# Attention with exponentials in transit: products with v a quarter slot later over three buffers, and norm statistics on POOL instead of VectorE

## The reference, cut to what matters

```
x = x + LN(attention(LN(x)))
x = x + LN(encoder_layer(LN(x)))       # 4-head attention over 8 positions, then 8 experts with capacity
```

```
q, k, v = relu(x Wq' + bq), relu(keys Wk' + bk), relu(values Wv' + bv)      # keys, values: shared by the batch
score   = q k' / sqrt(8)                                                    # 16 heads of width 8, 512 x 512
a       = softmax(score) v
a       = transpose(a, (0, 1, 3, 2)).reshape(8, 512, 128)                   # so 4 heads make 128 tokens
```

## Time and profile before

| | |
|---|---|
| three timed runs | 621.78, 622.29, 622.56 us; median 622.29 |
| the profiled execution | 623.81 us on the device, of which the span from first to last instruction is 621.3 |
| PE busy | 510.5 us, 82% |
| DVE busy | 526.5 us, 85% |
| ACT busy | 395.3 us, 64% |
| POOL busy | 194.5 us, 31% |
| row maxima, L1665 on DVE | 256 times 1220 ns |
| exponentials, L1597 on ACT | 512 times 604 ns |
| products with v, L1492 on PE | 1024 passes |

### The profile page before, as it was taken

How to read it: one execution, slowest core, us unless ns; L and a number is a source line. 1 busy time by engine, 2 the same in 40 slices (tenths; PEclk the granted TensorE clock), 3 DMA queues, 4 the chain that set the end, 5 groups by cost and what they waited for, 6 DMA issues and landing times.

```text
span 621.3 us, 9777 instructions
## 1 busy us (share of the span) xinstructions
PE 510.5 (82%) x3468; PEld 196.5 (32%) x3475; DVE 526.5 (85%) x879; ACT 395.3 (64%) x773; POOL 194.5 (31%) x309
## 2 busy tenths in 40 slices
PE   1794799999989999999999999877768798888520
PEld 1480122222222222222222222246547664433200
DVE  4769889999999999999999996157998769899976
ACT  1643378898989888888888988525446421144252
POOL 7000212039604544043461318329456330000000
PEclk9997589999999999999999999999988899999965
DMA  9943011111221112121112200010000000000012
GB/s 232 293 141 120 24 27 30 28 38 25 69 61 46 30 32 57 49 59 37 29 36 66 64 23 9 6 50 34 1 2 1 1 1 1 1 0 28 7 34 68
DMA packets 31392, 28.93 MB, mean 47 GB/s; under 512 B 6240, under 2 KB 23784, under 8 KB 31344
## 3 DMA queue, kind: packets, MB, share of 16 engines
q1 hardware_dynamic: 29312, 27.33, 15.1%
q10 hardware_dynamic: 2032, 0.98, 0.6%
HBM read 19.23 MB, written 8.65 MB: 45 GB/s over the span
## 4 chain that ended last, share of the span: by engine, by line
PE 45%; DVE 32%; POOL 7%; ACT 7%; issue 5%; DMA 2%; ACTq 1%; SPq 0%; DVEq 0%
PE ps L1492 14%; PE ps L1487 11%; DVE row_max L1665 10%; PE ps L1460 5%; DVE space L926 4%; PE ps L585 2%; DVE space L862 2%; ACT attended L1613 2%; ACT space L1597 2%; DMA w_in<-in_L_ffn_out_proj_w 1%; DVE st L233 1%; ACT space L830 1%; POOL space L402 1%; POOL space L404 1%; PE ps L342 1%
## 5 line engine op out<-in xcount | busy, mean ns | idle before, releaser
L1665 DVE TENSOR_REDUCE row_max<-ps 128x2 f32<-128x1024 f32 x256 | 299.5, 1220 | 17.0 <-PE ps L1460 14.2
L1597 ACT ACTIVATE space<-ps 128x512 f32<-128x512 f32 x512 | 271.8, 604 | 48.3 <-PE ps L1487 47.9
L1487 PE MATMUL ps<-space 51*128 51x512 bf16 x512 | 159.2, 388 | 7.0 <-ACT space L1597 3.3
L1492 PE MATMUL ps<-space 128*32 128x512 f32 x1024 | 138.1, 612 | 2.9 <-ACT space L1597 0.7
L1460 PE MATMUL ps<-space 48*128 48x512 bf16 x512 | 128.3, 400 | 14.2 <-DVE row_max L1665 12.5
L1487 PEld LDWEIGHTS ps<-space 51*128 51x128 bf16 x512 | 41.1, 94 | 165.1 <-ACT space L1597 144.6
L1333 POOL CAST max_parts<-row_max 128x16 bf16<-128x16 f32 x32 | 6.3, 198 | 236.8 <-DVE row_max L1665 236.8
L585 PE MATMUL ps<-W,space 128*128 128x512 f32 x128 | 66.7, 603 | 0.4
L926 DVE TENSOR_REDUCE space<-ps 128x128 f32<-128x1024 f32 x32 | 38.7, 1221 | 9.1 <-PE ps L585 8.8
L448 POOL TENSOR_TENSOR space<-PC,same_row 128x512 f32<-128x512 f32 x32 | 33.0, 1064 | 35.5 <-DVE PC L876 27.4
L1460 PEld LDWEIGHTS ps<-space 48*128 48x128 bf16 x512 | 26.4, 94 | 56.1 <-DVE row_max L1665 50.2
(11 more groups left out here) (216 smaller groups left out, 623.0 us busy)
## 6 DMA issues: line engine op xcount, KB each, us to landing
q_parts_dram<-space SPq DMA_DIRECT2D x2, 1536.0 KB, 5.4
space<-q_parts_dram SPq DMA_DIRECT2D x64, 48.0 KB
attended_dram<-attended SPq DMA_DIRECT2D x128, 18.0 KB
X<-in_L_attn_queries SPq DMA_DIRECT2D x8, 256.0 KB, 7.7
space<-in_L_ffn_w SPq DMA_DIRECT2D x2, 1024.0 KB, 5.9
space<-q_parts_dram SPq DMA_DIRECT2D x64, 32.0 KB
space<-attended_dram SPq DMA_DIRECT2D x16, 128.0 KB, 2.4
space<-inverses_dram SPq DMA_DIRECT2D x16, 128.0 KB
```

Of the source, the lines that this page charges most:

```text
L1487: pe.matmul(ps[:, col_bank(v), :], k_rows[rows_a, kappa // 4 % 2, tc * P:(tc + 1) * P], q_stack[rows_a, kappa % 4, b * S:(b + 1) * S], sta ...
L1492: mm = pe.matmul(ps[32 * m:32 * m + 32, PV, :], v_heads[:, tc, PAIR * (kappa // 4) + m % PAIR, :], probs[:, tc % 2, m, :], start=(tc == 0) ...
L1597: act.activation(probs[:, tc % 2, m, :], ps[:, col_bank(v), :], ACT.Exp, scale=1.0 / math.sqrt(DH)).then_inc(s_pr, 1)
L1665: dve.tensor_reduce(row_max[:, par].rearrange("p (a c) -> p a c", a=PAIR)[:, :, item], ring(n), AX.X, MAX).then_inc(s_free, 1)
```

## The change

Six things are changed.

1. `multiply_v` in a step multiplies the quarter before; after the last step one more call follows. The exponentials have three buffers, the third over `space8`.
2. ACT copies `attended` of slot kappa - 1 inside quarter 1 of slot kappa, between the third and the fourth exponential. Before, it did so after quarter 0.
3. SP issues `load_shift` before `store_attended` in each slot.
4. The statistics of groups 0 to 2 leave DVE. POOL sums 128 features by halving (`pool_add_up`: 7 additions), subtracts the mean, squares and sums again; a norm is spread over two slots (c = 4, 5 and 6, 7).
5. The addition of the output bias moves to the next slot c = 0, or behind the loop.
6. The turn of the first slot's maxima stands two pairs of rows earlier.

```diff
-        probs = view(space4, 0, [2, QB, S])
+        probs = [view(space4, 0, [QB, S]), view(space4, QB * S, [QB, S]), view(space8, 0, [QB, S])]
...
+        def pool_add_up(pool, ch, src, scratch, total):
+            n = D // 2
+            ch.done(pool.tensor_tensor(scratch[:, :, 0:n], src[:, :, 0:n], src[:, :, n:2 * n], ADD))
+            ch.wait()
+            while n > 2:
+                n //= 2
+                ch.done(pool.tensor_tensor(scratch[:, :, 0:n], scratch[:, :, 0:n], scratch[:, :, n:2 * n], ADD))
+                ch.wait()
+            ch.done(pool.tensor_tensor(total.rearrange("p (b o) -> p b o", o=1), scratch[:, :, 0:1],
+                                       scratch[:, :, 1:2], ADD))
+            ch.wait()
+        def pool_centre(pool, ch, src, dst, scratch):
+            mean = smallp[:, 0, :]
+            pool_add_up(pool, ch, src, scratch, mean)
+            ch.done(pool.tensor_scalar(mean, mean, 1.0 / D, None, MUL))
+            ch.wait()
+            ch.done(pool.tensor_tensor(dst, src, over_f(mean), SUB))
+            ch.wait()
+            ch.done(pool.tensor_tensor(scratch, dst, dst, MUL))
+            ch.wait()
+        def pool_scale(pool, ch, dst, scratch):
+            var, inv = smallp[:, 2, :], smallp[:, 3, :]
+            pool_add_up(pool, ch, scratch, scratch, var)
             ch.done(pool.tensor_scalar(var, var, 1.0 / D, EPS, MUL, ADD))
             ch.wait()
             ch.done(pool.tensor_tensor(inv, var, neg_half[:], ALU.pow))
             ch.wait()
             return pool.tensor_tensor(dst, dst, over_f(inv), MUL)
...
+                if kappa + 1 < NQ:
+                    sp.wait_ge(s_pr, turn_item(kappa + 1) + 1)
+                    load_shift(kappa + 1)
                 if kappa:
                     sp.wait_ge(s_pve, kappa)
                     store_attended(kappa - 1)
-                if kappa + 1 < NQ:
-                    sp.wait_ge(s_pr, turn_item(kappa + 1) + 1)
-                    load_shift(kappa + 1)
...
-                    if c == 5:
-                        pool_residual(pool, ch, g - 1)
-                    if c == 7:
-                        pool_input(pool, ch, g - 1)
+                    if c in (4, 5):
+                        pool_residual(pool, ch, g - 1, c - 4)
+                    if c in (6, 7):
+                        pool_input(pool, ch, g - 1, c - 6)
+                if g >= 2 and c == 0:
+                    pool_out_bias(pool, g - 2)
...
             for item in range(8):
-                if item == 4:
+                if item == 2:
                     pe.wait_ge(s_Wc, 2)
                     pe.wait_ge(s_csum, 1)
                     turn_max(0)
...
                 score_columns(kappa, tc + 1, 2)
-                if tc == 0 and kappa:
-                    pe.wait_ge(s_pve, kappa)
-                pe.wait_ge(s_pr, column_item(kappa, tc, QB - 1) + 1)
-                multiply_v(kappa, tc)
+                if kappa or tc:
+                    multiply_v(TC * kappa + tc - 1)
...
             for kappa in range(NQ):
-                for tc in range(1, TC):
-                    exps(kappa, tc)
-                    if tc == 1 and kappa + 1 < NQ:
-                        copy_turned(kappa + 1)
-                if kappa + 1 < NQ:
-                    exps(kappa + 1, 0)
-                act.wait_ge(s_pv, kappa + 1)
...
+                exps(kappa, 0)
+                exps(kappa, 1, range(QB - 1))
+                if kappa:
+                    copy_attended(kappa - 1)
+                exps(kappa, 1, range(QB - 1, QB))
+                if kappa + 1 < NQ:
+                    copy_turned(kappa + 1)
+                exps(kappa, 2)
+                exps(kappa, 3)
+            copy_attended(NQ - 1)
...
-                    if g and c == 4:
-                        dve_statistics(dve, s_r1, g - 1, A, tc)
-                    if g and c == 6:
-                        dve_statistics(dve, s_r2, g - 1, X, tc)
```

More of the change, by code:

```diff
@@ L412, in pool_divide, with pool_residual, pool_input, pool_out_bias @@
             pool.tensor_tensor(A[:, g], A[:, g], XN[:, g], ADD).then_inc(s_r1, 1)
[L414 to L423, removed]
+        def pool_residual(pool, ch, g, part):
+            if part == 0:
+                pool.wait_ge(s_r1, g + 1)
+                pool_centre(pool, ch, A[:, g], A[:, g], XN[:, g])
+            else:
+                ch.done(pool_scale(pool, ch, A[:, g], XN[:, g]))
+                ch.wait()
+                pool.tensor_tensor(X[:, g], X[:, g], A[:, g], ADD).then_inc(s_r2, 1)
+        def pool_input(pool, ch, g, part):
+            if part == 0:
+                pool.wait_ge(s_r2, g + 1)
+                pool_centre(pool, ch, X[:, g], A[:, g], XN[:, g])
+            else:
+                pool_scale(pool, ch, A[:, g], XN[:, g]).then_inc(s_n2, 1)
+        def pool_out_bias(pool, g):
             pool.wait_ge(s_n2, g + 1)
@@ L1542, in _ @@
                     step(kappa, tc)
+            multiply_v(TC * NQ - 1)
             back_end_pe(pe)
@@ L1591, in copy_turned, with exps, copy_attended @@
                 act.copy(max_turned[:, kappa % 2, :], src).then_inc(s_pr, 1)
-            def exps(kappa, tc):
-                for m in range(QB):
+            def exps(kappa, tc, which=range(QB)):
+                for m in which:
                     v = column_item(kappa, tc, m)
                     act.wait_ge(s_sc, v + 1)
-                    act.activation(probs[:, tc % 2, m, :], ps[:, col_bank(v), :], ACT.Exp,
+                    act.activation(probs[(TC * kappa + tc) % 3][:, m, :], ps[:, col_bank(v), :], ACT.Exp,
                                    scale=1.0 / math.sqrt(DH)).then_inc(s_pr, 1)
-            copy_turned(0)
-            exps(0, 0)
-            for kappa in range(NQ):
-                for tc in range(1, TC):
-                    exps(kappa, tc)
-                    if tc == 1 and kappa + 1 < NQ:
-                        copy_turned(kappa + 1)
-                if kappa + 1 < NQ:
-                    exps(kappa + 1, 0)
+            def copy_attended(kappa):
                 act.wait_ge(s_pv, kappa + 1)
@@ L1613, in _ @@
                 act.copy(attended[:, kappa % 2, :], ps[:, PV, :]).then_inc(s_pve, 1)
+            copy_turned(0)
+            for kappa in range(NQ):
+                exps(kappa, 0)
[8 more added lines that the diff above has]
+            copy_attended(NQ - 1)
             back_end_act(act)
```

35 lines of the change are left out of this document (11 added, 24 removed).

## The result

The changed kernel takes 626.56 us (median of 5 runs, 625.42 to 630.61), the kernel before 622.29 (5 runs, 621.78 to 624.05): a ratio of 1.0076, 95% interval 1.0044 to 1.0108. It is 4.3 us slower, where I forecast 622.6. The profiled execution took 630.61 on the device, its span is 628.7 and its mean granted clock (the share of TensorE's full clock) 0.932 (before: 623.81, 621.3 and 0.948). That execution is the slowest of the changed kernel on record, and has the lowest clock; the others took 625.42 to 627.44 at 0.941 to 0.946. So what follows is read from this one execution, and need not hold for the median.

The account below looks back on a forecast made before the run. The prediction took the chain PE - ACT - PE to bound the kernel, with no engine full. Its terms, -5.0 + 5.2 - 2.7 + 0.4 + 3.6 - 1.4 + 0.2 = +0.3, gave 622.6 us; 8-in-10 range 615.8 to 626.5.

Parts of the forecast that it names:

- Products a quarter later, -5.0: At each slot's first products PE no longer waits for the copy of bank 7: 31 times 0.16 us gained.
- the copy, +5.2: ACT's copy in quarter 1 delays the fourth exponential, so the turn's quarter grows from 2.61 to 2.79: 29 times 0.18 us.
- Rival B: In quarter 1 the copy hides in ACT's idle 0.33, so its +5.2 is 0: 617.4 us; chance 0.11.
- Statistics, -2.7: In the loop's norm slots, taking the statistics off DVE removes all their extra time, 2.7 us, if POOL keeps up.
- POOL, +0.4: In slots c = 4 to 7 POOL becomes full and its late splits delay the turn: 0.2 us for each of two groups.
- Rival C: POOL overflows in slots c = 4 to 7, its additions being slower than the straight line: 627.1 us; chance 0.15.
- Start, -1.4: Step 0 has no products, so the start is 1.9 us earlier, with 0.5 counted back for the low clock.
- Rival D: At the start the clock rises later, as PE has less to do, costing 1.4 us: 624.0 us; chance 0.12.
- SP's order and shift waits, +3.6: In SP's list loads wait for landed stores, so each of PE's three shift waits grows by 1.1 to 1.3 us.
- Rival A: PE's three waits for the shift vanish, making +3.6 into -2.8: 616.2 us; chance 0.18.
- End, +0.2: After the last exponential two quarters' products follow instead of one, so 2.07 us becomes 2.31.

Follow-up runs that it names:

- stores first: The changed kernel, but in slots c = 0 SP issues the stores ahead of the shift loads again; 621.34 us, ratio 0.9936 to the kernel before.
- SP's order alone: The kernel before with one edit: in every slot SP issues the shift loads ahead of the stores; 631.73 us, ratio 1.0144.
- products alone: The kernel before with three exponential buffers, products a quarter later, the copy's new place and the early first turn; 626.75 us, ratio 1.0023.
- split copy: The changed kernel with stores ahead of shift loads in slots c = 0, and half of bank 7's copy behind the turned chunk's copy; 620.79 us, ratio 0.9963.
- filler on POOL: The kernel before with statistics and output bias moved to POOL, plus 24 needless memsets on POOL in slot 4; 625.12 us, ratio 1.0029.
- filler on VectorE: The kernel before with statistics and output bias moved to POOL, plus 48 needless memsets ahead of VectorE's first wait; 621.09 us, ratio 0.9964.
- the statistics alone: The kernel before with only the statistics on POOL and the output bias moved; 625.35 us, ratio 1.0003.

## Why the prediction was wrong

- *Products a quarter later, -5.0, and the copy, +5.2.* Right in kind, 0.6 too low in sum. The 2.55 became 2.39 everywhere; the quarter with the turn is 2.81, not 2.79, so 29 of them cost 5.8. Rival B fell: had the copy been hidden, slots would be 9.78 (2.61 and three times 2.39).
- *Statistics, -2.7, and POOL, +0.4.* Right. Five slots of a group's norm work (202.98 to 253.03) take 50.05, so 0.15 over five clean ones, where 1.17 was before; the second group's went from 1.24 to 0.14 over, the last group's two slots from 0.26 to nothing. In all -2.4 net, where I had -2.3. Rival C fell: the turn is late by 0.1 per group, since additions of 512 to 8 elements lie on the line drawn, and the square takes 1.89, not 2.37.
- *Start, -1.4.* -1.86. Rival D fell: the clock rises at 81.9 (81.8 before).
- *SP's order and shift waits, +3.6: this step failed, in size.* "Each of the three waits grows by 1.1 to 1.3 instead of vanishing" is right for the waits themselves (+1.01, +1.29, +1.31, together 3.6; the waits are 6.4 in all, where I had 6 to 7). Rival A fell. What I left out is what a longer wait does to PE: I priced it at its own length, while in the profiled execution the clock fell behind each, another +4.0 behind the waiting quarters and most of 0.75 inside them. So the term is +8.4 there, not +3.6. Before, no wait of the loop had the low clock behind it, not the one of 1.43 either. But the low clock stood in the earlier trace rows, and I used it for the start alone.
- *How much of it is in the median is open.* The profiled execution is 4.05 us above the median. By my estimate its 13.7 us at half rate in the loop take 0.011 off the mean clock of 0.932, so the three executions at 0.946 (625.42 to 626.79) can hardly have had all of them, and they are still 3.1 to 4.5 us above the median of the kernel before. That the late shift causes the loss in the timed runs is shown (stores first, SP's order alone); how it divides there between low clock and the rest is not.
- *End, +0.2.* It does not show: from slot 29 to the last products it is 33.15 for 33.17.
- *Behind the loop* I had nothing. It is +0.95 in the profiles, and the statistics' move brought a fetched block of instructions into the last group's loads (the packet is there in the changed kernel too, at 9.8).

As measured, stretch by stretch, the loop is -1.86 + 0.3 - 0.1 - 1.6 + 8.6 = +5.3. With +1.2 ahead of it and +0.95 behind, the two profiled spans differ by 7.4, the medians by 4.3.

## What to carry to other kernels

A wait of TensorE that grows can cost more than its growth: look for the low clock behind it, and compare the mean clock of the profiled execution with that of the others before taking its loss for the usual one. When an order is changed so that one queue serves a wait sooner, ask what the moved instruction was itself the condition of: here the same SP queue served two deadlines in two slots, and the best order differs between them. Removing instructions can shift where an engine's later code is fetched, here into small loads that someone waits for (1 us); a before and after comparison of such work needs a filler of as many instructions.

## What the runs showed of the hardware

- The granted clock fell behind idle waits of PE of 2.44, 1.83 and 2.14 us (changed kernel), 1.85 and 1.51 (products alone), 2.51, 1.82 and 1.83 (SP's order alone), 1.62 (split copy) and also 1.32 (filler on POOL, slot 25, below). It did not fall behind 1.50 (filler on VectorE, slot 9), 1.43 (before), 1.24 (products alone), nor behind 1.39 with 1.46 of needless products ahead of it. So the length of the wait alone does not settle it; what else does is open.

```profile
337.76 0.39 PE L1510 MATMUL ps<-space 51*128 51x512 bf16 x2 [1.32 <-DMA space<-max_turned]
```

```profile
338.52:342.13 3.61, 3.61 (x18) 0.69 (x17) 1.81 (x2) 2.43 (x6) 0.83 (x4) 0.53 0.14 44
```

- The 8 KB instruction packet takes 0.55 to 0.70 us in this place in the seven kernels that have it, and in the run with the statistics alone the last eight 512-byte rows of the loads start only behind it. The Trainium skill, "DMA: Bandwidth & Descriptors", section "Queues, rings and completion order", says that a completion's semaphore write lands only after every earlier write of its DMA engine, across queues; DVE's wait of 2.46 against 1.44 us agrees, but does not test it, since here the data rows themselves start late.
- PE starts on the shift's two small loads 1.26 us after the end of their issue (five times 1.26 in the seven kernels of the table, 1.24 and 1.28 in the two others).
- POOL's additions take 1.27 us for 512 elements per partition, 0.46 for 128 and 0.20 for 8. Multiplying an operand by itself took 1.89 for 1024, and adding two different ones 2.37.
